# Sign convolution on image pairs: lower image halves crossed to the other image's partitions, with x loaded a second time for the sum

## The reference

```python
bw = cw + jax.lax.stop_gradient(jnp.sign(W) - cw)        # the sign of W
out = jax.lax.conv_general_dilated(x, bw, window_strides=(1, 1), padding=((1, 1), (1, 1)), ...)

def _gn(v, G=32, eps=1e-05):
    g = v.reshape(B_, G, C_ // G, H_, W_)
    return ((g - mean(g)) / jnp.sqrt(var(g) + eps)).reshape(v.shape)

x = x + conv(_gn(x), W)                                   # x: 32 x 64 x 56 x 56, W: 64 x 64 x 3 x 3
```

## Time and profile before

| what | value |
|---|---|
| runs | 223.40, 224.39, 224.81 us; median 224.39 |
| the profiled execution | 223.87 us, span 222.1 us |
| PE matmul | 196.0 us busy, 4658 instructions |
| DVE | 159.7 us busy |
| ScalarE | 140.7 us busy |
| POOL | 139.5 us busy |
| bytes | 25.95 MB read, 25.69 MB written |
| share of the 16 DMA engines, SP's queue | 64.8% |

### The profile page before, as it was taken

The page is one execution under the profiler, slowest core; times in us unless marked ns, Lnnn a source line. Parts: engine busy times, 40 slices in busy tenths (PEclk is TensorE's granted clock), DMA queues, the critical chain, the costliest instruction groups (busy, mean ns, idle before and its releaser), DMA issues.

```text
span 222.1 us, 10135 instructions
## 1 busy us (share of the span) xinstructions
PE 196.0 (88%) x4658; PEld 177.4 (80%) x4658; DVE 159.7 (72%) x336; ACT 140.7 (63%) x130; POOL 139.5 (63%) x69
## 2 busy tenths in 40 slices
PE   0049887989998999999999999999999999999990
PEld 0036576877887999999899999989898989899980
DVE  2509999769988677777677888878787777493443
ACT  2015568998959568493939495867768593929020
POOL 2453357997794947676775939495767676776330
PEclk9999999999999999999999999999999999999997
DMA  6999995407997957869593949495943333332526
GB/s 156 230 330 420 415 371 152 123 31 217 303 407 281 344 203 269 313 218 366 181 378 155 353 181 352 180 353 219 283 162 148 148 149 148 148 148 99 196 108 184
DMA packets 14778, 52.29 MB, mean 235 GB/s; under 512 B 1872, under 2 KB 1872, under 8 KB 14736
## 3 DMA queue, kind: packets, MB, share of 16 engines
q1 hardware_dynamic: 14496, 51.09, 64.8%
q10 hardware_dynamic: 240, 0.56, 1.1%
HBM read 25.95 MB, written 25.69 MB: 233 GB/s over the span
## 4 chain that ended last, share of the span: by engine, by line
PE 74%; DVE 13%; POOL 3%; ACT 3%; DMA 3%; issue 2%; ACTq 1%; DVEq 0%
PE psum L527 73%; DVE stats L364 5%; DMA w_raw<-in_L_conv_W_dram 3%; DVE xbuf L424 1%; POOL w_pos L257 1%; POOL w_raw L258 1%; ACT halves L310 1%; ACT xnorm L304 1%; DVE xbuf L432 1%; DVE stats L375 1%; POOL halves L269 1%; DVE own L380 1%; ACT moved L321 1%; DVE xnorm L404 1%; POOL w_sign L260 1%
## 5 line engine op out<-in xcount | busy, mean ns | idle before, releaser
L527 PE MATMUL psum<-halves,w_taps 64*64 64x385 f16 (+2 forms) x4608 | 191.7, 325 | 6.3 <-POOL halves L269 2.0
L527 PEld LDWEIGHTS psum<-halves,w_taps 64*64 64x64 f16 x4608 | 174.7, 107 | 23.8 <-issue 4.5
L269 POOL TENSOR_TENSOR halves<-xnorm,halves 128x1624 f16<-128x1624 f32 (+5 forms) x37 | 101.0, 2747 | 31.3 <-ACT xnorm L304 20.8
L364 DVE BATCH_NORM_STATS2 stats<-xbuf 128x6 f32<-128x448 f32 (+1 forms) x114 | 60.9, 603 | 4.8 <-DMA xbuf<-in_x_dram 4.8
L310 ACT ACTIVATE halves<-xbuf,coef 128x1624 f16<-128x1624 f32 (+5 forms) x38 | 56.6, 1490 | 2.4 <-DVE coef L395 2.0
L278 POOL TENSOR_TENSOR xbuf<-xbuf,moved 128x784 f32<-128x784 f32 x17 | 31.6, 1857 | 36.3 <-ACT moved L321 36.3
L424 DVE SCALAR_TENSOR_TENSOR xbuf<-psum,xbuf 128x784 f32<-128x784 f32 x31 | 30.1, 972 | 32.4 <-PE psum L527 32.4
L304 ACT ACTIVATE xnorm<-xbuf,coef 128x1624 f32<-128x1624 f32 (+5 forms) x36 | 52.6, 1504 | 0.0
L321 ACT ACTIVATE moved<-psum 64x784 f32<-64x784 f32 x34 | 27.8, 819 | 24.9 <-PE psum L527 24.3
L432 DVE SCALAR_TENSOR_TENSOR xbuf<-psum,xbuf 64x784 f32<-64x784 f32 x28 | 27.2, 973 | 0.9
L299 ACT ACTIVATE std<-own,eps 128x1 f32<-128x1 f32 x18 | 5.3, 294 | 30.3 <-DVE own L380 30.3
(11 more groups left out here) (24 smaller groups left out, 23.5 us busy)
## 6 DMA issues: line engine op xcount, KB each, us to landing
out_dram<-xbuf SPq DMA_DIRECT2D x56, 392.0 KB, 3.5
xbuf<-in_x_dram SPq DMA_DIRECT2D x14, 896.0 KB, 7.3
xbuf<-in_x_dram SPq DMA_DIRECT2D x14, 672.0 KB, 8.8
out_dram<-xbuf SPq DMA_DIRECT2D x16, 196.0 KB, 2.9
xbuf<-in_x_dram SPq DMA_DIRECT2D x7, 210.0 KB, 6.3
xbuf<-in_x_dram SPq DMA_DIRECT2D x7, 196.0 KB, 6.3
xbuf<-in_x_dram ACTq DMA_DIRECT2D x1, 210.0 KB, 3.3
xbuf<-in_x_dram ACTq DMA_DIRECT2D x1, 196.0 KB, 4.4
```

What stands on the lines that cost most here:

```text
L269: nc.gpsimd.tensor_tensor(at(halves[:, k % HRING, 1, :], a, b), at(xnorm[:, k % NRING, :], a, b), at(halves[:, k % HRING, 0, :], a, b), AL ...
L364: nc.vector.bn_stats(stats[:, k % 2, n, :], xbuf[:, k % XRING, a:b]).then_inc(blocks_ready, 1)
L527: mm = pe.matmul(outs[:, r0 - first:r1 - first, left:right], w_taps[lanes, t, :], ins[:, :, left + dx:right + dx], start=(half == 0 and n ...
```

## The change

All units become pairs: 16 of them, two groups each. Home is now the upper half of each image (rows 0 to 27) and away the lower half (rows 28 to 55). An away result is no longer brought back across the partition halves: the lower half of x is loaded a second time, into `crossed` (a ring of four), onto the partitions where the other image's away results stand, the sum is made there by one DVE instruction of 128 partitions, and it is stored from there. The copies to `moved`, POOL's additions, the paddings and the statistics' copies between partition halves go. Signs are made by one ScalarE instruction, the weights are first on ScalarE's queue, the fillers are 64. x is loaded four pairs ahead and the crossed half two pairs ahead. The first pair is cut into eight chunks, of which DVE makes the first two's parts, and the last group into phases of 7, 4 and 3 rows.

```diff
+AHEAD = 4
+SRING = 4
-WARM_UP = 8
-HEAD, TAIL = 3, 1
+WARM_UP = 16
...
+            cuts = [(first, 7, here), (first + 7, 4, here + 1), (first + 11, 3, (here + 2) % 4)]
+        phases += [Phase(e // 2, e, row, HALF + row, n, bank, 4 + bank) for row, n, bank in cuts]
...
+        if k == 0:
+            return [(0, 8), (27, 36), (8, 15), (36, 43), (15, 22), (43, 50), (22, 27), (50, 56)]
+        if k == 1:
+            return [(0, 15), (27, 43), (15, 27), (43, 56)]
         return [(0, 29), (29, 56)]
...
+        return [(0, 32), (32, 48), (48, 56)] if k == 0 else [(0, 32), (32, 56)]
...
+            def load_crossed(k):
+                for here, image in ((LOW, 2 * k + 1), (HIGH, 2 * k)):
+                    src = x[image:image + 1].rearrange("b c h w -> (b c) (h w)")
+                    sp.dma_start(crossed[here, k % SRING, :], at(src, HALF, H)).then_inc(crossed_loaded[k % SRING], 16)
...
+            for k in range(AHEAD):
+                for n in range(len(pieces(k))):
+                    start_load(sp, k, n)
+                if k < 2:
+                    load_crossed(k)
+            for k in range(NP):
+                new = k + AHEAD
+                if XRING <= new < NP:
+                    sp.wait_ge(stored[new % XRING], 32 * (new // XRING))
+                if new < NP:
+                    start_load(sp, new, 0)
+                for i in range(2):
...
+                    sp.wait_ge(home_done, e + 1)
+                    store(k, 14 * i, 14 * i + 14)
+                    sp.wait_ge(away_done, e + 1)
+                    store_crossed(k, HALF + 14 * i, HALF + 14 * i + 14)
+                    if i == 0 and new < NP:
+                        start_load(sp, new, 1)
+                    if i == 0 and k + 2 < NP:
+                        if k + 2 >= SRING:
+                            sp.wait_ge(crossed_stored[(k + 2) % SRING], 64 * ((k + 2) // SRING))
+                        load_crossed(k + 2)
...
-            nc.gpsimd.tensor_scalar(w_pos[:], w_raw[:], 0.0, -1.0, ALU.is_gt, ALU.add).then_inc(w_step, 1)
-            nc.gpsimd.tensor_scalar(w_raw[:], w_raw[:], 0.0, 0.0, ALU.is_ge, ALU.add).then_inc(w_step, 1)
-            pool.wait_ge(w_step, 2)
-            nc.gpsimd.tensor_tensor(w_sign[:], w_raw[:], w_pos[:], ALU.add).then_inc(w_step, 1)
...
-                nc.gpsimd.tensor_tensor(away, away, moved[:, m % 2], ALU.add).then_inc(add_done, 1)
...
-            start_load(act, 0, 1)
-            start_load(act, 0, 3)
             act.dma_start(w_raw[:], w.rearrange("o c h w -> o (c h w)")).then_inc(w_loaded, 16)
...
+            act.wait_ge(w_loaded, 16)
+            nc.scalar.sign(w_sign[:], w_raw[:]).then_inc(w_signed, 1)
...
-                    nc.scalar.mul(moved[here, m % 2], psum[there, bank:bank + 2, 0:BN], 1.0 / SCALE).then_inc(move_done, 1)
...
+            def add_away(e):
+                bank = 4 + 2 * (e % 2)
+                s = e // 2 % SRING
+                dve.wait_ge(crossed_loaded[s], 32 * (e // 2 // SRING + 1))
+                rows = at(crossed[:, s, :], 14 * (e % 2), 14 * (e % 2) + 14).rearrange("p (n m) -> p n m", m=BN)
+                nc.vector.scalar_tensor_tensor(rows, psum[:, bank:bank + 2, 0:BN], 1.0 / SCALE, rows,
+                                               ALU.mult, ALU.add).then_inc(away_done, 1)
...
+            for p in phases:
+                k, e = p.pair, p.group
+                ready = chunks_before(k) + chunks_for(p)
+                tiles = [(LOW, LOW, p.first, p.home), (HIGH, HIGH, p.first, p.home),
+                         (LOW, HIGH, p.away_first, p.away), (HIGH, LOW, p.away_first, p.away)]
...
+                        old = e - 1 if p.home // 2 != e % 2 else e - 2
+                        if old >= 0:
+                            pe.wait_ge(home_done, old + 1)
+                            pe.wait_ge(away_done, old + 1)
```

More of the change, by code:

```diff
@@ L20 @@
 NRING = 2
-WARM_UP = 8
-HEAD, TAIL = 3, 1
+AHEAD = 4
+SRING = 4
+WARM_UP = 16
 LOW, HIGH, ALL = slice(0, 64), slice(64, 128), slice(0, 128)
 @dataclass(frozen=True)
[L28 to L48, removed]
+class Phase:
+    pair: int
+    group: int
+    first: int
+    away_first: int
+    rows: int
+    home: int
+    away: int
 def conv_preact_kernel(nc: bass.Bass, x: bass.AP, w: bass.AP, out: bass.AP):
@@ L100, in chunks_before, with chunks_for, pieces @@
         return sum(len(chunks(i)) for i in range(k))
+    def chunks_for(p):
+        rows = {min(max(r, 0), H - 1) for a in (p.first, p.away_first) for r in range(a - 1, a + p.rows + 1)}
+        return 1 + max(n for n, (a, b) in enumerate(chunks(p.pair)) if rows & set(range(a, b)))
     EARLY = 2
[L105 to L127, removed]
+    def pieces(k):
+        return [(0, 32), (32, 48), (48, 56)] if k == 0 else [(0, 32), (32, 56)]
     with ExitStack() as ctx:
@@ L192, in start_load, with landed @@
[L192 to L196, removed]
+        def landed(k):
+            return 16 * (k // XRING + 1)
+        def start_load(eng, k, n):
+            a, b = pieces(k)[n]
+            eng.dma_start(at(xbuf[:, k % XRING, :], a, b), at(both(x, k), a, b)).then_inc(
+                loaded_third if n == 2 else loaded[k % XRING][n], 16)
@@ L198, in _ @@
         @block.sync
         def _(sp):
[L200 to L209, removed]
-                    dst = out[u.image:u.image + 2].rearrange("b c h w -> (b c) (h w)")
-                    sp.dma_start(dst[:, local * W:(local + n) * W],
-                                 xbuf[:, s, local * W:(local + n) * W]).then_inc(stored[s], 16)
-                    return
-                dst = out[u.image:u.image + 1].rearrange("b c h w -> (b c) (h w)")
-                for lanes, row in ((LOW, local - 1), (HIGH, local - 1 + HALF)):
-                    sp.dma_start(dst[:, row * W:(row + n) * W],
-                                 xbuf[lanes, s, local * W:(local + n) * W]).then_inc(stored[s], 16)
@@ new lines, in _ @@
+            for n, p in enumerate(phases[phases_before(LAST):]):
+                sp.wait_ge(home_done, LAST + 1 + n)
+                store(NP - 1, p.first, p.first + p.rows)
+                sp.wait_ge(away_done, LAST + 1 + n)
+                store_crossed(NP - 1, p.away_first, p.away_first + p.rows)
+            for k in range(NP - XRING, NP):
+                sp.wait_ge(stored[k % XRING], 32 * (k // XRING + 1) + (32 if k == NP - 1 else 0))
+            for k in range(NP - SRING, NP):
+                sp.wait_ge(crossed_stored[k % SRING], 64 * (k // SRING + 1) + (64 if k == NP - 1 else 0))
@@ new lines, in _ @@
+            for k in range(2):
+                pair_stats(k)
+                coefficients(k)
+                if k == 0:
+                    early_chunks()
+            for k in range(NP):
+                if k >= 1:
+                    add_home(2 * k - 1)
+                    add_away(2 * k - 1)
+                if 1 <= k < NP - 2:
+                    pair_stats(k + 2)
+                add_home(2 * k)
+                add_away(2 * k)
+                if k == 0:
+                    pair_stats(2)
+                if k < NP - 2:
@@ L471, in _ @@
                     coefficients(k + 2)
-            for j in range(2):
-                add_phase(NU - 1, j)
+            for n, p in enumerate(phases[phases_before(LAST):]):
+                add_phase(p, n)
         @block.tensor
```

316 lines of the change are left out of this document (99 added, 217 removed).

## The result

The changed kernel takes 232.6 us (median of four runs, 231.79 to 234.33), the kernel before 224.0 beside it: 1.039 times as long, with a 95% interval of 1.032 to 1.046. The forecast was 212.5, so it was wrong in sign. The profiled execution has a span of 232.4 us. Times here are medians of all runs, while ratios and intervals use only the runs of the faster of the two states in which a kernel can run, so the two can differ a little, as in experiments 3 and 5.

What follows compares the result with a forecast made beforehand. PE was taken as the bound, with a start, a convolution and an end: span 222.1 - 6.15 + 0.6 - 5.5 - 0.95 = 210.1 us, giving 212.5 us as time. Forecast 209 to 216 (0.55); 8 in 10 from 208 to 225.

Steps and rivals of the forecast that it cites:

- Stream: PE's convolution of sixteen pairs at 11.82 us, with +0.87 for the last phases: +0.6 us in sum, bounds +0 to +2.
- The sum into `crossed`: DVE's 128-partition sum of away results, priced like the one from `xbuf`: 0.97 us.
- The lead of ten us: Middle: crossed load lands near 36 us, is wanted at 46; eleven pairs eat 8 of the ten us spare.
- The share of 0.9 or more: Expected sign: a DMA share of 0.9 or more in the middle of the kernel, against 0.74 before.
- Start: Before the convolution: first matmul at 12.5 us instead of 18.65, -6.15 us; -2.3 if weights land at 8.3 as before.
- Stalls: PE's waits, mostly among the first units: 3 of 8.5 us kept, -5.5 us; bounds 1 to 6 us kept.
- Just hidden: 0: Middle: DMA needs 12.6 or 13.2 us per pair against PE's 11.82, but its early start covers this; no cost.
- End: After PE's last result: smaller last sums and earlier store issues, -0.95 us from 5.55.
- A: Middle: DMA becomes the bound at 13.7 to 14.4 us per pair, DVE waits for crossed loads; 230 us, chance 0.15.
- B: Middle: DMA sets 13.2 us per pair without loss from mixed traffic; 217.5 us, up to 222; chance 0.13.
- C: Start: weights land at 8.3 us as before, first matmul at 16.35; 216.5 us, chance 0.14 together with D.
- D: First pairs starve, PE's gaps before 50 us exceed 6; 4 us more, 216.5 us; chance 0.14 together with C.

Runs made afterwards that it cites:

- experiments 3: The kernel before plus an unused second load of x's lower half per pair, as one DMA of 128 partitions: 229.9 us, 1.014 of before.
- experiment 5: The changed kernel with each crossed load and store as one DMA of 128 partitions, the exchange of lower halves left out: 217.17 us, 0.960 of before.
- experiment 10: The kernel before with only the change's start: weights first, one sign on ScalarE, its own 32 fillers: 217.65 us, 0.972 of before.
- experiment 6: The changed kernel without the crossing (away results go back across the halves, x loaded once), with 32 fillers instead of 64: 211.12 us, 0.941 of before.
- experiment 4: The changed kernel without the crossing: away results go back across the halves as before, x loaded once, all DMAs of 128 partitions: 212.04 us, 0.942 of before.
- experiment 1: The changed kernel without the second load of x's lower half from the fifth pair on (output wrong): 219.51 us, 0.974 of before.

## Why the prediction was wrong, step by step

**What was right.** *Stream:* 220.21 less 208.39 between two home sums at the end is 11.82, the pace of the earlier trace rows; the four last groups show no gap. The last phases, expected to be held by weight loads at 1.93 us each, take 1.73 and 1.29 (between the last home sums, from DVE's timeline), so the +0.87 of this term was not due, and the bound +0 was the right one:

```profile
223.20 0.57 DVE L353 SCALAR_TENSOR_TENSOR xbuf<-psum,xbuf 128x392 f32<-128x392 f32 x1 [1.13 <-PE psum L426]
...
224.93 0.39 DVE L353 SCALAR_TENSOR_TENSOR xbuf<-psum,xbuf 128x224 f32<-128x224 f32 x1 [0.69 <-PE psum L426]
...
226.22 0.33 DVE L353 SCALAR_TENSOR_TENSOR xbuf<-psum,xbuf 128x168 f32<-128x168 f32 x1 [0.60 <-PE psum L426]
```

*The sum into `crossed`:* 965 ns, as priced. *The lead of ten us:* the crossed load is never late. But that is no test of the lead: from 13.6 to 226.2 us a pair takes 13.3 us on average, stalls included, no less than the 12.6 to 13.2 that DMA was priced at, so the queue had time that the forecast didn't give it. *The share of 0.9 or more* in the middle: 0.99 at 60 to 80 us, 0.84 to 1.01 in the stretches of 20 us up to 180.

**Start: right in kind, 1.1 us too early.** 13.6 instead of 12.5. From ScalarE's timeline of the changed kernel:

```profile
7.13 0.68 ACT L242 ACTIVATE w_sign<-w_raw 64x576 f16<-64x576 f32 x1 [4.23 <-DMA w_raw<-in_L_conv_W_dram]
```

The sign takes 0.68 us (0.85 was priced), but the weights land at 7.1, not 4.5: first on their queue wasn't first on the engines, on which a whole pair of x is under way. Where small pieces of x go first (experiment 10) the sign starts at 4.12; that the size of the pieces is the reason was not tested alone. The path of x was nearly as worked out: the coefficients end at 12.0 (11.6). The 64 fillers then hold PE to 13.6, as experiment 6 shows.

**Stalls: the step that failed, with "Just hidden: 0" of DMA.** I kept 3 us of stalls, with 0.9 for "a gap like that of the earlier trace rows". That gap was the sign of the mechanism. It stands at 69.4 us, at the end of a stretch in which the engines were full already in the kernel before, while the 0.74 of the earlier trace rows belongs to the stretch from 84 us on:

```profile
60.00:70.00 10.00, 9.42 (x227) 7.68 (x219) 8.82 (x19) 7.18 (x7) 7.46 (x3) 1.00 1.00 388
```

I carried it over as a constant while the same text worked out that the change fills the engines all the way. And "just hidden" asked only whether the *data* would be late. It wasn't; the instructions were. In place of 3 us stand 23.5. Where the crossed transfers are missing (experiments 4 and 6), PE keeps 3 us of gaps or less, so the estimate for the stalls among the first units was not the error.

**End: too small.** 6.2 us instead of 4.6. SP issues the crossed stores in pairs of 64 partitions and falls behind (timeline of SP):

```profile
224.27 2.56 SPq L177 DMA_DIRECT2D out_dram<-crossed  x2
...
229.49 1.11 SPq L177 DMA_DIRECT2D out_dram<-crossed  x2
```

The last pair of issues ends 4.4 us after PE's last result, not 2.0. With stores of 128 partitions (experiment 4: PE ends at 206.6 of 210.8) 4.2 are left.

**The rivals.** A gave 230 us and 0.15, and the time came out there, but not by its mechanism: no wait of DVE for the crossed load, and 11.82 us a pair at the end, where it had 13 and more to the last. B (217.5, up to 222), C and D (216.5) lie far below, and PE's gaps before 50 us come to 5.1, under D's mark of 6. Experiment 4, without the crossed transfers, takes 212.04, close to the forecast, but in part by luck: its first convolution comes at 14.24 instead of 12.5, 192.4 us pass from there to PE's end where 193.0 of stream and stalls were forecast, and the end takes 4.2 instead of 4.6.

**What the change is worth, in parts.** Start alone -6.6 us (experiment 10); pairs throughout with the last phases and without the crossing, at the same 32 fillers, another 6.5 (experiment 6 against 10); the crossed transfers, with the uncrossed sums that they buy, take back 20.6 (232.6 against 212.04), of which the second load from the fifth pair on is 13.1 (experiment 1). They buy nothing here, since the sums across the halves that they replace were off PE's path: in experiment 4 PE waits 0.6 us for another engine once the convolution runs.

## What to carry to other kernels

A transfer that nothing waits for can still cost time when it fills the DMA engines, since PE's own program comes over them: look at the instruction queue's packets and at "issue" gaps at equal counts of instructions, look at the DMA share of the few us before a gap and not at a mean, and treat one such gap before as a warning, not as a constant. Spend DMA share only where it takes work off the path that sets the end; here ScalarE, POOL and DVE had room for the crossing and the queue had not. If a transfer must go to both partition halves, one DMA of 128 partitions is far cheaper than two of 64 (217.2 us against 232.6), where the data allow it; experiment 5 leaves the exchange out, so it prices the shape and can't replace the change.

## What the runs showed of the hardware that was not expected

- PE's program comes in packets of some 16.5 KB, one for each 127 to 128 matmuls with their weight loads. At DMA shares of 0.72 to 0.84 (experiment 6) nearly all came in time; at 0.84 to 1.02 in the changed kernel a dozen were late, PE standing up to 2.3 us for one. A mean over a long stretch doesn't decide it: at 0.86 experiment 1 had no gap over 40 us, at 0.84 over 20 us the changed kernel had one of 2.32, right behind five us of full engines. In the Trainium skill, "Runtime: NRT & Kernel Launch", section "Instruction fetch mechanics" tells of blocks of 256 instructions over a queue of their own, fetched while the block before runs; the counts here agree. It takes the fetch to be mostly hidden; with the engines full it is not here, and the measurement decides.
- After a stand of two to four us PE can come back at the lower clock (granted clock 0.50): 3.4 us after two gaps of the changed kernel, 6.8 us in experiment 10. Gaps as long went without it, and what tells them apart no run here shows.
- Holding loads back to one at a time turned 5 to 6 us of landing for each into the pace of the kernel, 286 us.
